# Two sends of a chunk wait until the two of the chunk before have landed

## The reference

```python
x  = L0_attn_x
xn = _layernorm(x); x = x + L0_attn(xn) + L0_ffn(xn)   # ffn: 8 routed experts + a shared one
xn = _layernorm(x); x = x + L1_attn(xn) + L1_ffn(xn)   # ffn: two layers of local attention
xn = _layernorm(x); x = x + L2_attn(xn) + L2_ffn(xn)   # ffn: 8 routed experts
xn = _layernorm(x); x = x + L3_attn(xn) + L3_ffn(xn)
```

```python
topw, topi = top_k(softmax(xf @ router_w.T), 2)    # two experts for each row
xg   = xf[dispatch]                                # 8 x 640 rows, sorted by expert
eout = (silu(xg @ gate) * (xg @ up)) @ down        # of each expert
out  = zeros.at[dispatch].add(eout * weight)       # back to the rows
```

## Time and profile before

| | us |
|---|---|
| median of three executions | 4257.32 |
| lowest, highest | 4242.97, 4258.81 |
| span of the profiled execution | 4408.8 |

### The profile page before, as it was taken

One profiled execution on the slowest core, in us unless ns is written; L12 is line 12 of the kernel. 1 busy time (PEld: TensorE's weight loads), 2 busy tenths in 40 slices (PEclk: granted clock), 3 DMA queues, 4 the chain that ended last, 5 costly groups with the idle time before them and its releaser, 6 DMA issues. The chain is left out here.

```text
span 4408.8 us, 53684 instructions
## 1 busy us (share of the span) xinstructions
PE 3354.9 (76%) x20118; PEld 1509.9 (34%) x20182; DVE 2767.5 (63%) x4546; ACT 2535.5 (58%) x4166; POOL 1349.1 (31%) x1221
## 2 busy tenths in 40 slices
PE   7597788888968889989887897789868596631126
PEld 4265112222222222222222665466544273211125
DVE  5123889899755566556655775577566122488886
ACT  2112467767859989999996775477433222312225
POOL 1401183010011010010002884388311403228880
PEclk9698799999979989999998998899978798775558
DMA  4001121110020010010000111011020021550000
GB/s 137 33 19 52 36 49 33 30 33 16 2 62 23 7 29 15 15 29 1 15 1 16 33 33 33 17 34 36 14 81 11 28 64 31 78 61 0 10 6 24
DMA packets 140793, 137.36 MB, mean 31 GB/s; under 512 B 42568, under 2 KB 105844, under 8 KB 140532
## 3 DMA queue, kind: packets, MB, share of 16 engines
q1 hardware_dynamic: 130996, 116.08, 12.0%
q0 software_dynamic: 8192, 16.79, 1.6%
q10 hardware_dynamic: 1344, 1.05, 0.1%
HBM read 64.12 MB, written 33.82 MB: 22 GB/s over the span
## 5 line engine op out<-in xcount | busy, mean ns | idle before, releaser
L476 PE MATMUL PS<-t 50*128 50x512 bf16 (+2 forms) x3072 | 739.5, 398 | 205.9 <-ACT t L629 51.8
L609 ACT ACTIVATE t<-PS 128x512 f32<-128x512 f32 x1024 | 533.4, 605 | 243.0 <-PE PS L476 236.7
L748 DVE TENSOR_TENSOR t<-t 128x1536 f32<-128x1536 f32 (+1 forms) x384 | 584.8, 1592 | 124.7 <-ACT t L629 69.7
L664 DVE TENSOR_REDUCE t<-PS 128x1 f32<-128x1024 f32 x512 | 600.9, 1215 | 58.7 <-PE PS L468 40.5
L550 PE MATMUL PS<-t 128*9 128x512 f32 x4096 | 552.0, 612 | 10.9 <-DVE t L748 10.6
L631 ACT ACTIVATE t<-PS 128x1536 f32<-128x1536 f32 (+1 forms) x384 | 477.9, 1312 | 53.7 <-PE PS L476 37.2
L629 ACT ACTIVATE t<-PS 128x1536 f32<-128x1536 f32 (+1 forms) x384 | 477.3, 1313 | 35.6 <-PE PS L476 23.5
L476 PEld LDWEIGHTS PS<-t 50*128 50x128 bf16 (+2 forms) x3072 | 158.9, 94 | 988.8 <-ACT t L629 272.4
L468 PE MATMUL PS<-t 48*128 48x512 bf16 x1024 | 342.4, 405 | 45.2 <-DVE t L664 24.5
L1823 POOL TENSOR_TENSOR t<-t 128x512 f32<-128x512 f32 x128 | 159.7, 1269 | 577.1 <-ACT t L1688 576.5
L2639 PE MATMUL PS<-t 128*128 128x32 f32 x256 | 61.1, 403 | 344.8 <-ACT t L2685 281.3
(11 more groups left out here) (402 smaller groups left out, 6380.9 us busy)
## 6 DMA issues: line engine op xcount, KB each, us to landing
t<-scr SPq DMA_DIRECT2D x336, 64.0 KB
t<-t SPq DMA_DIRECT2D x128, 128.0 KB, 2.3
scr<-t SPq DMA_DIRECT2D x96, 128.0 KB
t<-t SPq DMA_DIRECT2D x16, 512.0 KB, 12.6
scr<-t SPq DMA_DIRECT2D x2, 2560.0 KB
t<-scr SPq DMA_DIRECT2D x16, 320.0 KB, 3.6
scr<-t SPq DMA_DIRECT2D x16, 320.0 KB, 2.7
t<-scr SPq DMA_DIRECT2D x48, 48.0 KB
```

Source lines behind the costliest of these rows:

```text
L476: return e.op.matmul(PS[:, bk, :], Kx[p // 4 % 2][lo:lo + rows, j, kb * 128:kb * 128 + 128], Qx[p // 4 % 2][lo:lo + rows, j, hf * 512:hf * ...
L609: e.op.activation(P[x % 4][:, 2 * hf + side, :], PS[:, bank((what, p, k, side, hf)), :], ACT.Exp, scale=S8).then_inc(*PW.up((p, k, side, hf)))
L664: e.op.tensor_reduce(MX[p % 2][:, side, qc:qc + 1], PS[:, 2 * side:2 * side + 2, :].rearrange("p a n -> p (a n)"), AX, ALU.max).then_inc(* ...
L748: e.op.tensor_tensor(o, o, SGM[(12 * p + 3 * blk + ti) % 3][:, 0:nu, :], ALU.mult).then_inc(*DG.up((p, blk, ti)))
```

## The change

In `send`, from the second chunk on, POOL waits before the two sends of a chunk until both sends of the preceding chunk have landed. The semaphore is the same, and so is its last count; its counts are now named by chunk. Both mixtures call `send`, so it holds for both.

```diff
                 e.wait_ge(GZ, "zeros")
                 for ch in range(NC):
+                    if ch:
+                        e.wait_ge(SENT, ("rows", ch - 1))
                     for dst, src, w in self.picks:
                         e.op.indirect_dma_start(
                             GX, bass.IndirectOffsetOnAxis(ap=dst[:, ch:ch + 1], axis=0), XN[:, ch, :],
-                            None).then_inc(*SENT.up("rows", 16))
+                            None).then_inc(*SENT.up(("rows", ch), 16))
```

## The result

The change makes the kernel slower by 0.93%: 4295.99 us (median of four executions, 4287.05 to 4298.23) against 4254.53 (four: the three known before and one of 4251.75 us; 4242.97 to 4258.81), ratio 1.0093 [1.0077, 1.0109]. That is 41.5 us; 42 were forecast. The profiled execution took 4298.23 us, 1.8 more than its span.

The account below looks back on a forecast made before the run. PE is busiest, but 147.0 us of stalls beside sends and gathers were read as the recording's. Exposed sends of 4.1 us (layer 0) and 36.4 (layer 2) plus 1.5 for the clock, 42 on 4257.3, gave 4299 us, range 4240 to 4345.

Parts of the forecast that it names:

- The period: POOL's sends in both mixtures: a chunk with the wait takes 3.95 us (3.45 to 4.74) in place of 2.53.
- the landing and POOL's waking: Two terms of a chunk's period: 1.3 us until the second send lands, 0.29 us until POOL issues again.
- The tail: End of the sends in both layers: SP, waiting for them at the start of `experts`, goes on with the last landing.
- Layer 0: Sends end at 222.6 us; the shared expert, ending at 218.5, hides all but 4.1 us (0 to 29.3).
- Layer 2: Sends end at 3519.4 us, the attention without stall at 3483.0: 36.4 us exposed (20.4 to 61.7).
- The clock: Start of layer 2's `experts`: PE's clock falls while it waits, adding 1.5 us (0 to 3).
- The choice that decided the sign: Stalls beside both layers' sends and layer 2's gathers, 147.0 us, come with the recording; timed executions hardly have them.
- The forecast of the profile after: Both send stalls gone, the gathers' stalls untouched; profiled span falls by up to 74.5 us to about 4334.
- the clearest proof of the choice: The pair of signs: profiled span falls, by up to 74.5 us, while the timed executions get slower.
- The first rival: Both layers' send stalls are real and the wait ends them: 74.5 us saved, 4183 us; chance 0.14.
- The second rival: A part of the stalls is real, 25 to 50%: no change, 4258 us; chance 0.10.
- The third rival: Send stalls are real, last as long as the sends and grow by 56%: slower, 4322 us; chance 0.06.

Follow-up runs that it names:

- the kernel before (again): The kernel before, unedited, run and profiled a second time on a first chip: 4257.98 us against 4255.98, ratio 1.0004; its recorded execution took 4249.26.

## Why the prediction was right, and where it was not

The change comes out 41.5 us slower where 42 was forecast. The steps:

- **The period.** Forecast 3.95 us, measured 3.75, nearly all of it in two terms: the landing and POOL's waking together are 1.53 us, where 1.3 + 0.29 was taken, and the first send after a wait took 0.96, not 1.10. From the start of a send to its landing the trace gives 2.2 us. The Trainium skill agrees with that: "DMA: Bandwidth & Descriptors", in its section on the anatomy of a DMA issued by GpSimd, fits 2.0 us plus the bytes at 436 KB/us, an estimate of 2.15 us for 64 KB.
- **The tail.** I let SP start 1.3 us after the last issue, with the landing. It starts 5.52 us after it, before the change and after. That is the time to the end of the DRAIN behind POOL's list. This term was missed altogether. By luck it and the shorter period cancel: in layer 0 first send to fetches takes 124.6 us (126.1 forecast), in layer 2 129.2 (128.1).
- **Layer 0.** Its end was forecast at 222.6 and came at 222.78, with 218.54 before (218.5). Of the 4.2 us between them 2.6 are the waits, and the terms give just that: without waits the last send of the kernel before (again) is issued from 176.29 to 177.25, the tail ends at 182.8, and the addition at 218.26 leaves 35.5 us of slack, while 31 waits of 1.23 us are 38.1. The rest is that this execution's sends began later.
- **Layer 2.** 36.4 us forecast, measured 36.3 as the stage's length and 36.8 timed alone. The agreement to 0.1 us is luck, since the single terms were less good. Without stalls the attention ended 89.5 us after the first send (3397.89 - 3308.41), 91.7 by my sum (3483.0 - 3391.3). And sends meet DVE's large products already in the kernel before: the 64 take 87.4 us (3395.78 - 3308.41), where 79.7 + 0.96 was the sum of layer 0. I had added 2 us for that on the side of the change alone.
- **The clock.** 1.5 us forecast, nothing found: the first expert's matmuls take 10.83 us after and 11.24 in the kernel before again.
- **The choice that decided the sign** was right in its conclusion, that the timed executions don't have the stalls, and wrong in its reason. I read 147.0 against 151.5 us as the recorder's price. Recorded executions without stalls (4249.26 us for the kernel before, all three stretches of the kernel after) and 25 timed ones of about 4404.6 show that it isn't recording as such that tells the two kinds apart, but the chip or its moment. Whether the recorder has a part in it where they stall isn't shown: the record has a span and a granted clock for every timed execution as well, so none is known to have run without it. By the Trainium skill, "NOTIFIC — the notification-queue block", section 7.1, a filling queue of records can hold an engine back; no run here shows the queue, for or against. What the numbers most likely said is that the profile of before and its three timed executions came from unlike chips: 4408.8 + 1.8 = 4410.6 lies inside 4395.39 to 4410.7, and 4257.32 inside 4244.48 to 4271.59.
- **The forecast of the profile after.** A fall to "about 4334" was expected, with the stall at the gathers left; the span is 4296.4, and that stall is gone as well. Both follow from a profile taken where nothing stalls. As "the clearest proof of the choice" it was worthless: the pair of signs came, and its reason was another.
- **The first rival** was the more right one in its mechanism. On a chip with stalls a pair of sends per landing does end them: 61.0 us in layer 0 (61.7 in the rival), 10.1 in layer 2 (12.8), 71.1 together by the traces and 80.8 timed (74.5). On such a chip its sign would have been the right one. The second rival, a part of the stalls in every execution, finds no support: the medians lie at 4254 to 4260 us or at 4404.6, with nothing between. The third rival, stalls that grow with the sends, is wrong: with 2.5 us for a send there are none.

Open: what stalls the other engines, and why on one chip and not on three. Sends 1.26 us apart stall, pairs per 3.75 us and singles per 2.5 us don't. Whether the rate decides it or the moments without a transfer under way isn't known: the kernels with spacing and no wait for a landing met only chips without stalls. The change in its exact form wasn't run on a chip with stalls, only with the one wait more at its end; nor were the waits in layer 0 alone. By their terms that last form would give the 61 us there and cost 0 to 7 us elsewhere, which would make it the best of both. That is worked out, not measured.

## What to carry to other kernels

When the profiled span and the timed median differ by a few per cent, first ask whether they are of the same chip, and profile the unchanged kernel again before explaining the difference. A wait for a transfer is priced by what is behind it: here 31 waits of 1.53 us cost 3 us where the engine's list had 35.5 us of slack and 36 us where it had none. And look at how long after an engine's last instruction its stage really ends, since that tells whether there is slack at all.

## What the runs showed of the hardware that was not expected

- On one chip of four, and in the profile of before, 64 indirect DMAs of POOL, 1.27 us apart, went with late handovers from PE to ACT and DVE: PE busy for 22 to 23 of 68 us, and ACT and DVE taking turns 5.60 us apart in place of 0.86. The same kernel took 4256, 4257 and 4260 us on three chips and 4404.6 on the other.
- A stage that waited for POOL ended 5.5 us after POOL's last instruction, an indirect DMA or a memset, with the end of a DRAIN on POOL's queue 0.2 us before it, and 7.0 us after the last indirect DMA when POOL waited for its landing first.
- An execution's time was its span plus 1.76 to 1.95 us in every one on record.
